# A decoder layer on one core: the shared expert's down projection as products of rounded parts, and GpSimd takes the rest of ctx

## What is computed

```
q = xpos(x @ Wq);  k = xpos(ctx @ Wk, inverse);  v = ctx @ Wv
x = layernorm(x + ((q @ k.T) * decay) @ v)
shared = (silu(x @ gate) * (x @ up)) @ shared_down      # inner size 512
out = layernorm(x + shared + combined)                  # two of eight experts for each row
```

## Time and profile before

| | us |
|---|---|
| median of 3 runs | 1873.14 (1871.34 to 1873.53) |
| the profiled execution | 1876.15 |
| its span, with a mean granted clock of 0.963 | 1874.4 |
| TensorE busy | 1713.3 |
| VectorE busy | 1179.4 |
| ScalarE busy | 802.0 |
| GpSimd busy | 719.2 |

### The profile page before, as it was taken

One profiled execution on the slowest core, in us unless ns is written; L12 is line 12 of the kernel. 1 busy time (PEld: TensorE's weight loads), 2 busy tenths in 40 slices (PEclk: granted clock), 3 DMA queues, 4 the chain that ended last, 5 costly groups with the idle time before them and its releaser, 6 DMA issues.

```text
span 1874.4 us, 35484 instructions
## 1 busy us (share of the span) xinstructions
PE 1713.3 (91%) x9524; PEld 1435.8 (77%) x9525; DVE 1179.4 (63%) x2682; ACT 802.0 (43%) x1491; POOL 719.2 (38%) x625
## 2 busy tenths in 40 slices
PE   6999996999965999999999987999999999999980
PEld 4666655888864888888888875888888888888870
DVE  6777766888854667667677666555555555555546
ACT  5677766777721332322323334333333333333326
POOL 1011105888851243544435446233332333333333
PEclk9999997999996999999999998999999999999995
DMA  4444455777824222222122225333333333333329
GB/s 138 174 173 174 159 199 178 234 245 244 264 102 139 91 84 89 81 92 103 69 82 100 80 97 192 59 53 57 55 55 58 52 57 54 55 58 52 58 43 358
DMA packets 137705, 220.64 MB, mean 118 GB/s; under 512 B 40544, under 2 KB 110368, under 8 KB 129328
## 3 DMA queue, kind: packets, MB, share of 16 engines
q1 hardware_dynamic: 112064, 184.44, 30.1%
q0 software_dynamic: 25584, 35.54, 10.9%
HBM read 122.79 MB, written 97.12 MB: 117 GB/s over the span
## 4 chain that ended last, share of the span: by engine, by line
PE 44%; DMA 11%; issue 5%; POOL 5%; DVE 3%; ACT 2%; SPq 0%; POOLq 0%; ACTq 0%; another core or an unknown queue 0%; DVEq 0%
PE back_ps L2476 13%; DMA acc<-back_y,back_token 10%; PE back_ps L2496 7%; PE back_ps L2378 5%; PE back_ps L2364 4%; PE back_ps L2355 3%; PE back_ps L2274 3%; POOL back_turned_qk L1727 2%; POOL sorted L1715 2%; PE back_ps L2485 2%; PE back_ps L2309 2%; ACT back_out L1895 2%; PE back_ps L2317 2%; PE back_ps L2296 1%; PE back_ps L2262 1%
## 5 line engine op out<-in xcount | busy, mean ns | idle before, releaser
L2476 PE MATMUL back_ps<-back_w_gu,back_xe_T 128*128 x1620 | 413.0, 404 | 1.3 <-DVE back_xe_T L2212 1.3
L1758 POOL DMA_INDIRECT acc<-back_y,back_token x135 | 209.0, 1548 | 461.6 <-DVE back_y L2231 364.0
L2476 PEld LDWEIGHTS back_ps<-back_w_gu,back_xe_T 128*128 128x128 f32 x1620 | 297.5, 189 | 61.3 <-issue 2.3
L2496 PE MATMUL back_ps<-back_w_down,back_he_T 128*128 x1620 | 225.4, 288 | 1.5 <-DVE back_he_T L2224 1.5
L2496 PEld LDWEIGHTS back_ps<-back_w_down,back_he_T 128*128 128x128 f32 x1620 | 200.8, 189 | 1.8 <-issue 1.7
L1179 PE MATMUL front_ps<-front_xn_T,front_w_in_parts 128*128 128x512 f32 x768 | 186.6, 399 | 5.2 <-issue 3.3
L1715 POOL DMA_INDIRECT sorted<-back_x,back_slot x128 | 136.6, 1067 | 134.6 <-DVE back_slot L2044 100.3
L1010 DVE SCALAR_TENSOR_TENSOR front_conv<-front_ps,front_conv_wb,front_conv 128x508 f32<-128x508 f32 (+2 forms) x192 | 141.2, 742 | 63.4 <-ACT front_conv L842 58.9
L1179 PEld LDWEIGHTS front_ps<-front_xn_T,front_w_in_parts 128*128 128x128 f32 x768 | 143.3, 190 | 48.5 <-issue 18.5
L2220 DVE TENSOR_TENSOR back_h<-back_h,back_ps 128x512 f32<-128x512 f32 x135 | 92.7, 687 | 119.5 <-PE back_ps L2476 119.5
L1889 ACT ACTIVATE back_he_T<-back_ps 128x512 fp32r<-128x512 f32 x135 | 80.7, 598 | 200.2 <-PE back_ps L2485 200.2
(11 more groups left out here) (230 smaller groups left out, 3031.2 us busy)
## 6 DMA issues: line engine op xcount, KB each, us to landing
back_xe<-sorted SPq DMA_DIRECT2D x135, 136.0 KB, 2.5
gate_T<-front_gate_T SPq DMA_DIRECT2D x16, 1024.0 KB, 4.7
xc_T<-front_xc_T SPq DMA_DIRECT2D x16, 1024.0 KB, 5.7
front_xc_in<-xc_T SPq DMA_DIRECT2D x16, 1024.0 KB, 5.5
front_gate_in<-gate_T SPq DMA_DIRECT2D x16, 1024.0 KB, 6.5
front_x_rows<-in_x SPq DMA_DIRECT2D x16, 512.0 KB, 5.5
front_c_rep<-c_parts SPq DMA_DIRECT2D x128, 64.0 KB, 4.1
front_rows_in<-in_x SPq DMA_DIRECT2D x16, 512.0 KB, 7.3
```

Of the source, the lines that this page charges most:

```text
L1758: pool.indirect_dma_start(out=d["acc"][:, :], out_offset=bass.IndirectOffsetOnAxis(ap=token[:, r:r + 1], axis=0), in_=y[:, r % 2], in_offs ...
L2476: op = nc.tensor.matmul(dst[:, r % 2], xe_T[:, x_part, k], w_gu[:, bass.ds(e, 1), m, w_part, k], start=(n == 0), stop=(n == len(PASSES) - 1))
L2496: op = nc.tensor.matmul(ps_y[:, 0:D_MODEL], he_T[:, h_part, k], w_down[:, bass.ds(e, 1), w_part, k], start=(n == 0), stop=(n == len(DOWN_P ...
```

## The change

The hidden chunk stays float32 only in a buffer of two chunks, `h_T`, into which both silu and its product with up are written. ScalarE rounds each chunk to `h_high`, VectorE subtracts for `h_low`; `w_down_s` is split in the first step. The down projection becomes three products for each pair of chunk and sequence, chunk by chunk: the chunks 0 and 1 of all four sequences ahead of the turn of the next x1, 2 and 3 behind it. `c_raw` now lies where the rest of c goes, so that the subtraction works in place and the load waits for `k_done`; GpSimd does the subtraction, after four scatters; ScalarE's `round_c` moves between silu 1 and silu 2. `v` and `base` share a buffer, so the copy of v waits for the store of `base`. At the end, w_down[2] is loaded and rounded after `down_done`.

```diff
         x1 = at("x1", 140, [P, GS, D_MODEL])
-        c_raw = at("c_raw", 144, [P, KM, GT])
-        v = at("v", 148, [P, GS, D_MODEL])
-        scores_T = at("scores_T", 152, [P, GT])
-        sum_rows = at("sum_rows", 154, [P, GS, D_MODEL])
+        v = base = at("v", 152, [P, GS, D_MODEL])
+        c_raw = at("c_raw", 76, [P, KM, GT])
+        scores_T = at("scores_T", 156, [P, GT])
+        sum_rows = at("sum_rows", 198.75, [P, GS, D_MODEL])
         tables = {n: at(n, 158 + i / 2, [P, P]) for i, n in enumerate(("q_cos", "q_sin", "k_cos", "k_sin"))}
...
         x2_T = at("x2_T", 112, [P, 2, KM, GT], F32R)
-        h_T = at("h_T", 120, [P, KF, GT])
+        h_high = at("h_high", 120, [P, KF, GT], F32R)
+        h_low = at("h_low", 180.5, [P, KF, GT], F32R)
 
...
         x2 = at("x2", 172, [P, 2, GS, ROW])
-        base = at("base", 180.5, [P, GS, D_MODEL])
-        silu_T = at("silu_T", 184.5, [P, 2, GT])
-        w_down_s = at("w_down_s", 188.5, [P, KF, D_MODEL])
+        h_T = at("h_T", 144, [P, 2, GT])
+        w_down_s = [at("w_down_s_high", 188.5, [P, KF, D_MODEL], F32R), at("w_down_s_low", 148, [P, KF, D_MODEL], F32R)]
+        w_down_s_raw = at("w_down_s_raw", 148, [P, KF, D_MODEL])
         ident = at("ident", 192.5, [P, P])
...
         owner = at("owner", 194.0625, [1, SLOT_TILES], I32)
-        small = 204.25
+        small = 204.75
         router = at("router_parts", small, [P, KM, 2, EXPERTS], F32R)
-        logits_T = at("logits_T", 202.25, [2 * EXPERTS, GT])
+        logits_T = at("logits_T", 202.75, [2 * EXPERTS, GT])
         logits = at("logits", small + .125, [P, GS, EXPERTS])
...
         h_ready = sem("h_ready")
+        h_high_ready = sem("h_high_ready")
+        h_low_ready = sem("h_low_ready")
+        w_down_s_high_ready = sem("w_down_s_high_ready")
+        w_down_s_ready = sem("w_down_s_ready")
         down_done = sem("down_done")
...
                 sp.dma_start(raw_of[name], d[name].rearrange("p k f -> p (k f)")).then_inc(w_loaded[name], 16)
-            sp.dma_start(w_down_s, d["shared_down"]).then_inc(w_down_s_loaded, 16)
+            sp.dma_start(w_down_s_raw, d["shared_down"]).then_inc(w_down_s_loaded, 16)
             sp.wait_ge(w_ready, SPLIT.index("W_k") + 1)
...
                     if not is_at(a, GROUPS - 1):
-                        sp.wait_ge(c_T_ready, a + 1)
+                        sp.wait_ge(k_done, 2 * (a + 1))
                         sp.dma_start(c_raw, d["ctx_T"][a + 1]).then_inc(c_loaded, 16)
...
                         sp.wait_ge(x2_ready, GS * GROUPS)
-                        load_w_down(0, 1, 2, 3)
+                        load_w_down(0, 1, 3)
                         load_chunks(11, 12, 13, 14)
...
                         sp.wait_ge(down_done, GROUPS)
-                        sp.wait_ge(base_stored, 16 * (GROUPS - 1))
-                        load_w_down(7)
+                        load_w_down(2, 7)
                     else:
...
                         in_=x2[:, u, s], in_offset=None).then_inc(scattered[u], 16)
+
+            def rest_c(a):
+                pool.wait_ge(c_high_ready, a + 1)
+                nc.gpsimd.tensor_tensor(c_T[:, 1], c_raw, c_T[:, 0].bitcast(F32), ALU.subtract).then_inc(c_T_ready, 1)
+
+            rest_c(0)
 
...
                     scatter(expert[0] - 1, 1 - expert[1], 1)
+                if attention and not is_at(a, GROUPS - 1):
+                    rest_c(a + 1)
                 if attention:
...
             in_steps(pool, step)
-            for e in (2, 3):
+            for e in (3, 2):
                 pool.wait_ge(w_down_high_ready[e], 1)
...
 
+            def round_h(g, i):
+                act.wait_ge(h_ready, KF * g + i + 1)
+                if i == 0 and not is_at(g, 0):
+                    act.wait_ge(down_done, g)
+                nc.scalar.activation(h_high[:, i], h_T[:, i % 2], ACT.Copy).then_inc(h_high_ready, 1)
+
             high_of("W_q")
...
                         act.wait_ge(attended, a)
+                    if not early(a):
+                        act.wait_ge(base_stored, 16 * (a - 1))
                     nc.scalar.activation(v, ps_rows, ACT.Copy).then_inc(v_ready, 1)
...
                         nc.scalar.activation(x2_T[:, 0, k], ps_turn[:, k], ACT.Copy).then_inc(x2_high_ready, 1)
-                if attention and not is_at(a, GROUPS - 1):
-                    act.wait_ge(k_done, 2 * (a + 1))
-                    round_c(a + 1)
                 if expert and attention and u:
...
                         nc.scalar.activation(probs, logits, ACT.Sigmoid).then_inc(probs_ready, 1)
+                    if i == 2 and attention and not is_at(a, GROUPS - 1):
+                        round_c(a + 1)
                     if expert:
...
                         if i:
-                            act.wait_ge(h_ready, KF * g + i - 1)
-                        nc.scalar.activation(silu_T[:, i % 2], ps_wide[:, (2 * i + 2) % 3], ACT.Silu).then_inc(silu_ready, 1)
+                            act.wait_ge(h_low_ready, KF * g + i - 1)
+                        nc.scalar.activation(h_T[:, i % 2], ps_wide[:, (2 * i + 2) % 3], ACT.Silu).then_inc(silu_ready, 1)
+                        if i:
+                            round_h(g, i - 1)
                     if i == 1 and is_at(expert and g, GROUPS - 1):
...
                         chunk_high(11)
+                if expert:
+                    round_h(g, KF - 1)
                 if is_at(expert and g, GROUPS - 1):
...
                     chunk_high(13)
-                    w_down_high(2)
+                    act.wait_ge(base_stored, 16 * (GROUPS - 1))
                     w_down_high(3)
...
                     w_down_high(4)
+                    w_down_high(2)
                     w_down_high(7)
...
                         high_of(name)
+                    act.wait_ge(w_down_s_loaded, 16)
+                    nc.scalar.activation(w_down_s[0], w_down_s_raw, ACT.Copy).then_inc(w_down_s_high_ready, 1)
 
...
                                             ALU.subtract).then_inc(x1_T_ready, 1)
-
-            def rest_c(a):
-                dve.wait_ge(c_high_ready, a + 1)
-                nc.vector.tensor_tensor(c_T[:, 1], c_raw, c_T[:, 0].bitcast(F32), ALU.subtract).then_inc(c_T_ready, 1)
 
...
                 dve.wait_ge(silu_ready, KF * g + i + 1)
-                if not is_at(g, 0) and i == 0:
-                    dve.wait_ge(down_done, g)
-                nc.vector.tensor_tensor(h_T[:, i], silu_T[:, i % 2], ps_wide[:, 2 * i % 3],
+                nc.vector.tensor_tensor(h_T[:, i % 2], h_T[:, i % 2], ps_wide[:, 2 * i % 3],
                                         ALU.mult).then_inc(h_ready, 1)
+
+            def rest_h(g, i):
+                dve.wait_ge(h_high_ready, KF * g + i + 1)
+                nc.vector.tensor_tensor(h_low[:, i], h_T[:, i % 2], h_high[:, i].bitcast(F32), ALU.subtract
+                                        ).then_inc(h_low_ready, 1)
 
...
             rest_x1(0)
-            rest_c(0)
             low_of("W_v", 2)
...
                     add_bias(g)
-                if attention and not is_at(a, GROUPS - 1):
-                    rest_c(a + 1)
                 if expert:
...
                     hidden(g, 1)
+                    rest_h(g, 0)
                     if not attention:
...
                     hidden(g, 2)
+                    rest_h(g, 1)
                     if not attention:
...
                     hidden(g, 3)
+                    rest_h(g, 2)
                 if attention:
...
                 if expert:
+                    rest_h(g, 3)
                     if not attention:
...
                         low_of(name, 4 + n)
+                    dve.wait_ge(w_down_s_high_ready, 1)
+                    nc.vector.tensor_tensor(w_down_s[1], w_down_s_raw, w_down_s[0].bitcast(F32), ALU.subtract
+                                            ).then_inc(w_down_s_ready, 1)
                 if expert and not attention:
...
 
-            def down(g, ahead, first):
-                if is_at(g, 0):
-                    pe.wait_ge(w_down_s_loaded, 16)
-                if first == 0:
-                    pe.wait_ge(h_ready, KF * g + KF - 1)
+            def down(g, ahead, chunks):
+                if is_at(g, 0) and 0 in chunks:
+                    pe.wait_ge(w_down_s_ready, 1)
+                if 0 in chunks:
                     pe.wait_ge(sum_ready, 2 * (g + 1 + ahead))
-                for s in (first, first + 1):
-                    for i in range(KF):
-                        if s == 0 and i == KF - 1:
-                            pe.wait_ge(h_ready, KF * (g + 1))
-                        op = nc.tensor.matmul(ps_rows[:, s], h_T[:, i, seq(s)], w_down_s[:, i], start=(i == 0),
-                                              stop=(i == KF - 1))
-                if first:
+                for i in chunks:
+                    pe.wait_ge(h_low_ready, KF * g + i + 1)
+                    for s in range(GS):
```

(9 more changed lines are left out.)

## The result

The changed kernel takes 1882.78 us (median of 5 runs, 1881.79 to 1883.29) against 1873.53 us before, measured beside it (1871.34 to 1874.12): ratio 1.0047, 95% interval 1.0033 to 1.006. It is slower by 9.25 us. Its profiled execution took 1881.79 us, with a span of 1880.1. In the experiment with one more subtraction, one of four runs took 3072.3 us at a mean granted clock of 0.705 and is left out of its figures.

What follows compares the result with a forecast made beforehand. VectorE's chain and TensorE end the tail within 0.34 us, so added VectorE work shows. 14 x (0.9 - 0.6) = 4.2, last tail 1.2, clock 3.4: + 8.8 us, 1882 from the 1873.14 median; range 1868 to 1897.

Steps and rivals of the forecast that it cites:

- the likeliest case: Whole kernel: slower, at 1882 us, its own range 1878 to 1890; chance 0.45.
- The tail: Down projection's start to next query projection: VectorE's two added rests cost 1.20 us, less 0.34 slack, about 0.9 later.
- the last tail: Tail of group 14, without x1: the whole + 1.2 us shows.
- The head: Query projection to score products: waits for turned keys and logits go, 0.6 us per group on the mean.
- TensorE's 18 us: Down projection in rounded parts: 1.14 us less TensorE work per group, 18 us in 16 groups, a gain only if alone on the path.
- GpSimd's rest of ctx against the rest of h chunk 1: Ahead of hidden(3): GpSimd's subtraction delays VectorE's rest, by 0.98 us or until 869.0, with 0.9 us left by the rows.
- the rival in which GpSimd's rest of c comes late: Ahead of hidden(3) or in the tail: VectorE held up to 2.43 us per group; 1896 with 1 us; chance 0.13.
- The clock: After TensorE's new pauses of 2.0 us: two falls of the granted clock, 1.7 us each, + 3.4 us.
- a fall in each group: Upper bound of the clock term: one fall in each of 14 groups, 24 us, 1902; as a rival, chance 0.10.
- The sum: Whole kernel: 4.2 for 14 groups, 1.2 last tail, 3.4 clock, + 8.8 us, which makes 1882.
- Buffers and queues: Load of ctx and copy of v, with their new waits: taken as 0, upper bound 2.4 us in every second group.

Runs made afterwards that it cites:

- this half of the change by itself: The kernel before with only the rest of ctx on GpSimd and its rounding between silu 1 and 2, float32 products kept: 1864.91 us, ratio 0.9957.
- with the rest of ctx placed better too: The changed kernel with rests of h chunks 2 and 3 on GpSimd and the rest of ctx on VectorE behind the decay of the scores: 1861.59 us.

## Why the prediction was right

The direction, the likeliest case and the time held. The terms did not all, and the sum is close partly because their errors cancel.

**The tail: right.** Forecast + 0.9 us for two rests at 0.60 us less 0.34 us of slack; measured + 0.88, with rests at 0.60 and 0.57. TensorE's new pause, forecast at 2.0 us, was 1.35 to 1.92 in twelve groups and 0.83 in two. That it is VectorE's chain was shown four times: without the two rests (7.8 us), with them on GpSimd (7.8), with one more (9.77), and with less work for TensorE (no change). In the last tail the whole 1.2 us was forecast, and the turn of x2 came 1.18 us later; the stall ahead of it grew from 0.43 to 2.00 us.

**The head: right.** Forecast - 0.6 as the upper bound, measured - 0.72, and - 0.70 for this half of the change by itself. But 0.10 us comes back behind the scores in both kernels, so that this half takes 33.84 - 33.23 = 0.61 us off a group, the forecast's number. (The other 0.09 us by which every second group grew behind the scores no term had.) The turned keys take 2.55 us, the number forecast, and the wait at the logits is 0.35 us in every group. The half alone was worth about 8 us, 14 x 0.6 being 8.4. My reason was a little off: GpSimd need not take the work, it is enough that the subtraction and the rounding leave their places in the head.

**TensorE's 18 us: right that they are hidden.** TensorE did lose 18.1 us of busy time. Behind VectorE's chain they only lengthen TensorE's pauses.

**GpSimd's rest of ctx against the rest of h chunk 1: right, and the rows alone would have been short.** It started 5.0 us behind the end of the turned keys (829.42 to 834.40), as worked out, and took 2.38 us. VectorE's rest beside it lost 1.83 - 0.68 = 1.15 us, not 0.98. It ended 0.55 us behind GpSimd's, which lost nothing. The row in the third group (3.56 us, its end 0.56 us behind GpSimd's) and the pick of 1.27 us show the same. They agree with the rule quoted in the prediction (the Trainium skill, SBUF — State Buffer, SBUF: two separate sides), that a VectorE operation with two SBUF inputs waits for the whole instruction of GpSimd. Which of the two comes first is less plain than the rule has it, which gives the shared ports to whichever starts first: in the third group VectorE's record starts 0.59 us ahead of GpSimd's, and VectorE waits all the same.

The slip of the rival in which GpSimd's rest of c comes late did happen, but in one group and not in fourteen. The distance of that group to the next is 34.83 us, and 34.03 with the rest of ctx on VectorE; this 0.8 is most of the 1.0 us by which the groups' + 5.2 exceeds the forecast + 4.2.

**The clock: the step that failed.** I took two falls in the groups behind pauses of 2 us, + 3.4 us. There was none behind 14 pauses of 0.83 to 1.92 us, so this term measured nothing in the groups. In the last step the fall was 6.83 us long instead of 3.40, but TensorE had made it up by the ranks behind it (0.04 us). Nor is its length the change's doing for certain: the kernel with the rests on GpSimd had a fall of 6.83 us there in one profiled execution and of 3.41 in the other, and its last stretch (from the last query projection to the first tile) was 0.4 us longer in the first. The bound, a fall in each group, was not idle: with the pauses at about 2.00 us four of 14 groups had a fall in one experiment and three in another, at 1.6 us each.

**The sum: right in part by luck.** Forecast + 4.2 for the groups, + 1.2 for the last tail and + 3.4 for the clock, + 8.8; in the trace the groups made + 5.2 and the last stretch + 3.4, together + 8.6. What the clock did not cost, two things did that no term had: the third group's slip (0.8), and in the last stretch 2.2 us beyond the 1.2 of the tail. There the last scatter took 2.61 us more to land. Why is not known: with the rest of ctx on VectorE the turn of the last x2 is as late (34.08), the landing as long (5.26 us), and yet the last stretch is only 1.3 us longer than before. Two stretches that the change hardly touches, the front and the experts' tiles, were together 3.0 us shorter in the profiled execution, which makes + 5.6. The medians differ by 9.25. The profiled execution of before (1876.15) lies above all its timed runs, that of after is as low as the lowest of its own. The forecast of 1882 therefore owes some of its closeness to the runs as well; the + 8.8 lies within the measured interval of 6.2 to 11.2 us.

**Buffers and queues: costed at nothing, and right.** The copy of v starts at 853.99, 0.12 us behind the last value product and 4.7 us behind the issue of the store of base (849.28), and the trace shows no wait for that store. The load of ctx is issued at 857.66 in this group; such loads take 3.3 us to land (the median), and ScalarE asks at 865.73.

**Open.** What tells a pause of 2.00 us with a fall behind it from one without was not found. What makes the last stretch 2.2 us longer than the forecast tail is not known. Nor was it shown why the kernel with a third of the products left out has its three falls in the early groups. It was also not tried whether the wait for x1's load, 7.5 us in all, goes if sum_rows is let through earlier.

## What to carry to other kernels

When two engines' chains end 0.34 us apart, taking 18 us of work from the one can win no more than that gap in each group until the other gives way. Ask of every added instruction which chain it is in, and put it on the engine whose chain has room, though that one is twice as slow for it. Split a change that touches two places before you judge it: one half here was worth 8 us, the other cost about 17. With its two rests moved the second half costs nothing any more (1864.91, the same as the first half alone), and with the rest of ctx placed better too the kernel is at 1861.59 against 1872.16; the first half was not run with that last move alone, so how much of the 3 us is the products' is open. And keep GpSimd's subtractions from meeting VectorE's with two SBUF inputs on the path, the smallest ones included.

## What the runs showed of the hardware that was not expected

A VectorE operation of 32 elements (0.19 us) took 1.27 us beside a GpSimd subtraction of 1.28 us: the one that waits lost 1.08 us here and 1.15 us in an operation of 128x512, so the loss does not scale with its own work.

Pauses of TensorE of one length at one place of the program did not all have a fall of the granted clock to 0.50 behind them. With one more subtraction, four of ten pauses of 2.00 us had one; with a third of the products left out, one of ten, and beside it the pauses of 1.99 and 2.14 us. Such a fall lasted 3.41 us and cost 1.6 us, though TensorE was at work in all of it.

A product of float32 operands of this shape shows as two records, 16 in 3.61 us for eight products. The three products of rounded parts for each of the same eight show as 24 in 2.97 us. That is 0.45 us against 0.37 for one product of 128x256, so three for one is a gain here.
